# A fused transformer block on Trainium2: in its cross-attention stage, scores placed right behind attention, and one attention block moved into the next step

## The chip, the cores and the metric

One NeuronCore of a Trainium2 chip runs the whole block as one program. The metric is the device time of the program in microseconds (us); lower is better. Several executions of the kernel before were timed, and one more was recorded by the hardware profiler.

## The reference, cut to what matters

The block has three stages, each added to x (64 batches of 64 tokens, 512 wide, all float32): cross-attention over a context of 512 tokens, self-attention with 16 heads, and a feed-forward layer with ternary weights.

```python
x = x + xattn(layernorm(x), ctx, ctx, mask, W_Q, W_K, W_V, W_O)
x = x + attn(layernorm(x), Wq, bq, Wk, bk, Wv, bv, Wo, bo)
x = x + ffn(layernorm(x), W1, b1, W2, b2)

def xattn(Q, K, V, mask, W_Q, W_K, W_V, W_O):   # 16 heads of 32
    q, k, v = Q @ W_Q.T, K @ W_K.T, V @ W_V.T   # split into heads
    e = einsum('bhqd,bhkd->bhqk', q, k) / sqrt(32)
    e = where(mask, -inf, e)                    # mask: True is left out
    a = einsum('bhqk,bhkd->bhqd', softmax(e), v)
    return a @ W_O.T
```

The mask given leaves only keys of the last 128 of each batch's 512, and the kernel finds this out at run time (a flag) and then works with the last tile of 128 keys alone. The change is in the cross-attention stage; the other two stages are the same before and after.

## The kernel before, in words

**Tiling.** The cross stage has 16 units of 4 batches (4 x 64 = 256 tokens, two tiles of 128). A step `step(u, kind)` finishes the attention of unit u and, beside it, projects keys, values and queries of the next unit v = u+1. Steps 0 to 14 do both (`more` is true); step 15, the last, has no next unit. `run_steps` (L107) writes steps 0, 1, 14 and 15 out and runs the others as a loop of two steps a round.

**Precision.** Every projection is done with operands split into a high and a low part, so one output bank (128x512) takes 12 matmuls: 4 chunks of the contraction by the products hi*hi, hi*lo and lo*hi (`split_products`, whose matmul is L331). They are called here K0 to K3 (keys), V0 to V3 (values, one a batch), Q0 and Q1 (queries, 24 narrower matmuls each) and O0 and O1 (output projections of unit u's two tiles). They share two PSUM banks `project` in turn; a fixed list of names (`Banks`, with `full` at L437 and below) says which use gets which bank, and each use waits until the last use of its bank has been read out (`pj_free`).

**The attention of one batch q** goes through all compute engines:

- TensorE `scores(u, q)`, L581: 32-row tiles, 16 matmuls in the program (32 records in the trace), into PSUM `scores`.
- VectorE `maxima(u, q)`: adds the mask into SBUF (L842, which frees the PSUM), row maxima (L847), the bias of the exponential (L852).
- ScalarE `exponentials(u, q)`, L730: eight exponentials with row sums.
- VectorE `divide(u, q)`, L397 and L401: reciprocal of the sums and one product over 128x1024.
- TensorE `transposes(u, q)`, L590: eight transpositions into `probs_t_psum`.
- ScalarE `probs_t_out(u, q)`, L741: copy to SBUF.
- TensorE `attend(u, q)`, L607: 32-column tiles, into `attended_t`. Batches 0 and 1 fill tile 0, batches 2 and 3 tile 1.
- per tile, ScalarE `a_hi` (L715) and VectorE `a_lo` (L827) split the attended tile, TensorE does O0 or O1, VectorE `residual` (L864) adds it to x, and SyncE stores it (L515).

**Order.** There is no scheduler: each engine has its own list of calls in `step`, done strictly in that order, and semaphores tie them together. On TensorE (L620) one full step before is:

```
scores 0, O1 of u-1, K0, scores 1, K1, transposes 0, K2, attend 0, K3, scores 2,
V0, transposes 1, V1 with scores 3 in its middle, attend 1, V2, transposes 2,
O0, attend 2, Q0, transposes 3, Q1, attend 3, V3
```

On VectorE (L874): maxima 0, residual of O1 (u-1), divide 0, maxima 1, statistics of the next x, divide 1, `x_lo`, maxima 2, values_out V0, maxima 3, values_out V1, divide 2, a_lo 0, values_out V2, divide 3, residual of O0, split of the context of u+2, a_lo 1, values_out V3. `values_out` (L833) empties the bank of a V projection. On ScalarE (L750): exponentials 0, keys_out 0 and 1, probs_t_out 0, exponentials 1, keys_out 2, `x_hi`, keys_out 3, probs_t_out 1, exponentials 2, a_hi 0, exponentials 3, probs_t_out 2, split of the context, queries_out 0, probs_t_out 3, queries_out 1, a_hi 1. SyncE (L485) loads context and x^T of u+2, stores the two finished tiles, and then loads x of u+2 (L475) once the stores have landed, since both use the same buffer. GpSimd only works out the scale of the logits.

Of the kernel before, what the change touches and what calls it, by code (L numbers as in the profile page):

```python
# [43 lines left out]
def later(u, n):  # L44
    return Unit(u.half, u.off + n)
# [10 lines left out]
def is_unit(u, n):  # L56
    return isinstance(u.half, int) and number(u) == n
# [62 lines left out]
def build(nc, x, x_t, ctx, mask, w_cross, w_self, bq, bk, bv, bo, w1, b1, w2, b2,  # L120
# [4 lines left out]
    with outer:  # L125
# [261 lines left out]
        def self_w_lo(e, n):  # L387
            e.wait_ge(sw_hi_ready, n + 1)
            nc.vector.tensor_tensor(flat_w(sw_lo, n), s_stages[n],
                                    flat_w(sw_hi, n).bitcast(F32), ALU.subtract) \  # L390
                .then_inc(sw_lo_ready, 1)
# [143 lines left out]
        def cross_pe(e, K):  # L535
# [84 lines left out]
            def step(u, kind):  # L620
                more, ahead = kind != "last", kind == "full"
                v = later(u, 1)

                if is_unit(u, 0):
                    bank, before = K.banks.at(None, "Q1")
                else:
                    bank, before = K.banks.at(later(u, -1), "Q1",
                                              "last_but_one" if kind == "last" else "full")
                e.wait_ge(C.pj_free[bank], before + 1)
                scores(u, 0)  # L630
                if is_unit(u, 0):

                    e.wait_ge(w_lo_ready, 4)
                else:

                    o_proj(later(u, -1), K.nt - 1, "last_but_one" if kind == "last" else "full")
                if more:
                    k_proj(u, v, 0)
                scores(u, 1)
                if more:  # L640
                    k_proj(u, v, 1)
                    transposes(u, 0)
                    k_proj(u, v, 2)
                    attend(u, 0)
                    k_proj(u, v, 3)
                    scores(u, 2)
                    v_proj(u, v, 0)
                    transposes(u, 1)
                    v_proj(u, v, 1, lambda: scores(u, 3))
                    attend(u, 1)  # L650
                    v_proj(u, v, 2)
                    transposes(u, 2)
                    if K.nt == 2:
                        o_proj(u, 0, kind)
                    attend(u, 2)
                    q_proj(u, v, 0)
                    transposes(u, 3)
                    q_proj(u, v, 1)
                    attend(u, 3)
                    v_proj(u, v, 3)  # L660
                else:
                    scores(u, 2)
                    transposes(u, 0)
                    scores(u, 3)
                    attend(u, 0)
                    transposes(u, 1)
                    attend(u, 1)
                    transposes(u, 2)
                    if K.nt == 2:
                        o_proj(u, 0, kind)  # L670
                    attend(u, 2)
                    transposes(u, 3)
                    attend(u, 3)
                    o_proj(u, K.nt - 1, kind)
# [21 lines left out]
        def cross_act(e, K):  # L696
            def full(u, name, kind="full"):

                bank, before = K.banks.at(u, name, kind)
                wait(e, C.pj_full[bank], before + 1)  # L700
                return bank

            def keys_out(u, v, m):
                bank = full(u, f"K{m}")
                nc.scalar.activation(ck_t[:, parity(v), m, :, :].rearrange("p j k -> p (j k)"),
                                     PJ[bank][:], ACT.Copy).then_inc(C.pj_free[bank], 1)

            def x_hi(v):
                wait(e, xt_in, total(v, 16 * K.b, 16 * K.b))
                flat = lambda a: a[:, 0:K.b].rearrange("p b c s -> p (b c s)")  # L710
                nc.scalar.activation(flat(cxt_hi), flat(cxt_raw), ACT.Copy).then_inc(C.xt_hi, 1)

            def a_hi(u, t):
                wait(e, C.pv_done, total(u, 4, 4 // K.nt * (t + 1)))
                nc.scalar.activation(cat_hi[:, :, 0:K.tp], K.attended_t(t), ACT.Copy) \  # L715
                    .then_inc(C.at_hi, 1)

            def queries_out(u, n):

                bank = full(u, f"Q{n}")  # L720
                chunks = PJ[bank][:].rearrange("p (i b s) -> p i b s", i=2, s=SEQ)
                nc.scalar.activation(cq_t[:, 2 * n:2 * n + 2, 0:K.b, :], chunks[:, :, 0:K.b, :],
                                     ACT.Copy).then_inc(C.pj_free[bank], 1)

            def exponentials(u, q):
                wait(e, C.s_bias, total(u, 4, q + 1))
                width, buf = K.kt * P, q % 2
                for g in range(PAIRS // K.kt):
                    cols = slice(g * width, g * width + width)
                    last = nc.scalar.activation(  # L730
                        c_p[buf][:, cols], c_s[buf][:, cols], ACT.Exp,
                        bias=exp_bias[:, buf, g:g + 1],
                        scale=logit_scale[:, parity(u), K.batch(q):K.batch(q) + 1],
                        accum_out=c_row_sum[:, buf, g:g + 1])
                last.then_inc(C.p_ready, 1)

            def probs_t_out(u, q):
                wait(e, C.pt_full, total(u, 4, q + 1))

                wait(e, C.pv_done, total(u, 4, q))  # L740
                nc.scalar.activation(c_pt[:], PT[:], ACT.Copy).then_inc(C.pt_ready, 1)  # L741

            def split_ctx(v):

                wait(e, ctx_in[parity(v)], total_of_parity(v, 64, 64))
                nc.scalar.activation(ctx_hi[:, parity(v)].rearrange("p j c k -> p (j c k)"),
                                     ctx_raw[:, parity(v)].rearrange("p j c k -> p (j c k)"),
                                     ACT.Copy).then_inc(ctx_hi_ready, 1)

            def step(u, kind):  # L750
                more, ahead = kind != "last", kind == "full"
                v = later(u, 1)
                exponentials(u, 0)
                if more:
                    keys_out(u, v, 0)
                    keys_out(u, v, 1)
                probs_t_out(u, 0)
                exponentials(u, 1)
                if more:
                    keys_out(u, v, 2)  # L760
                    x_hi(v)
                    keys_out(u, v, 3)
                probs_t_out(u, 1)
                exponentials(u, 2)
                if K.nt == 2:
                    a_hi(u, 0)
                if not more:
                    self_w_hi(e, 0)
                    probs_t_out(u, 2)
                exponentials(u, 3)  # L770
                if more:
                    probs_t_out(u, 2)
                else:
                    self_w_hi(e, 1)
                if ahead:
                    split_ctx(later(u, 2))
                if more:
                    queries_out(u, 0)
                else:
                    self_w_hi(e, 2)  # L780
                probs_t_out(u, 3)
                if more:
                    queries_out(u, 1)
                a_hi(u, K.nt - 1)

            first = Unit(0, 0)
            split_ctx(first)
            cross_w_hi(e, 1)
            keys_out(None, first, 0)
            keys_out(None, first, 1)  # L790
            x_hi(first)
            keys_out(None, first, 2)
            keys_out(None, first, 3)
            cross_w_hi(e, 2)
            cross_w_hi(e, 3)
            queries_out(None, 0)
            queries_out(None, 1)
            split_ctx(later(first, 1))
            run_steps(e, K.units, step)

        def cross_dve(e, K):
# [72 lines left out]
            def step(u, kind):  # L874
                more, ahead = kind != "last", kind == "full"
                v = later(u, 1)
                maxima(u, 0)
                if not is_unit(u, 0):
                    residual(later(u, -1), K.nt - 1, "last_but_one" if kind == "last" else "full")
# [36 lines left out]
                if not more:  # L916
                    self_ln_statistics(e, Unit(0, 0))
                    e.wait_ge(G.stats, NT)
                    self_ln_normalise(e, Unit(0, 0))
                a_lo(u, K.nt - 1)  # L920
                if more:
                    values_out(u, v, 3)
                else:
                    self_w_lo(e, 2)
                    residual(u, K.nt - 1, kind)

# [884 lines left out]
```

## Time and profile before

| | before |
|---|---|
| median of 3 runs | 1789.76 us (1788.92 to 1798.7) |
| profiled execution | 1789.14 us |
| its span, first to last instruction | 1787.3 us |
| mean granted TensorE clock | 0.981 |
| TensorE busy | 1697.0 us, 95% |
| TensorE weight load busy | 1424.1 us, 80% |
| VectorE busy | 1030.4 us, 58% |
| ScalarE busy | 703.0 us, 39% |
| GpSimd busy | 205.4 us, 11% |

The time of an execution is a little longer than its span (1789.14 against 1787.3 us), because the span begins at the first instruction and ends with the last. The cross stage takes some 784 us of it, self-attention up to about 1150, the feed-forward layer the rest. In the rows, PE is TensorE's matmul, PEld its weight load, DVE VectorE, ACT ScalarE, POOL GpSimd and SPq SyncE's DMA queue. A timeline row has start and length in us, the engine, the line of the kernel, the operation, output<-inputs, shapes and count, and in brackets the engine's idle time before it with what ended that. The chain of work that ended last follows the program back from its last instruction, at each step to what released it, or else to the instruction before it on its engine.

### The profile page before, as it was taken

The page shows a single profiled execution, that of the slowest core. Times are in us where ns is not written, and L with a number is a line of the kernel's source. Part 1 is how long each engine was busy: PE and PEld are TensorE (multiplying, and loading weights), DVE is VectorE, ACT ScalarE, POOL GpSimd, SP SyncE. Part 2 cuts the span into 40 slices and gives each one's busy share as a digit, 9 for nine tenths or more (in the row PEclk, how much of TensorE's full clock was granted, in tenths as well). Part 3 has the DMA queues.
Part 4 walks back from the last instruction along what each step waited for, and adds up shares of the span by engine and source line. Part 5 has one row for each costly group of instructions (what it writes and reads, how often), then busy time and mean ns, then how long its engine had stood idle before and what let it go on. Part 6 is the DMA issues. An engine that isn't in the chain of part 4 may idle for free.

```text
span 1787.3 us, 38867 instructions
## 1 busy us (share of the span) xinstructions
PE 1697.0 (95%) x16268; PEld 1424.1 (80%) x16268; DVE 1030.4 (58%) x1494; ACT 703.0 (39%) x1689; POOL 205.4 (11%) x298
## 2 busy tenths in 40 slices
PE   6899999999999999769999999999699999999999
PEld 4788878888888788558889888988578888888887
DVE  3655555555555555546677776778654455445533
ACT  3555555555555555536422222222122222222221
POOL 1000000000000000011112121211121022102200
PEclk9999999999999999879999999999799999999999
DMA  5011111111111111241010101000211011101000
GB/s 213 13 60 61 60 61 60 61 60 61 60 61 60 61 60 72 95 189 50 25 50 25 47 26 43 32 25 34 66 36 48 1 48 48 47 0 47 24 24 24
DMA packets 48695, 95.45 MB, mean 53 GB/s; under 512 B 5792, under 2 KB 14112, under 8 KB 47264
## 3 DMA queue, kind: packets, MB, share of 16 engines
q1 hardware_dynamic: 48544, 93.16, 14.9%
q8 instruction: 128, 2.10, 0.5%
q14 instruction: 23, 0.19, 0.0%
HBM read 67.97 MB, written 25.17 MB: 52 GB/s over the span
## 4 chain that ended last, share of the span: by engine, by line
PE 90%; DVE 4%; issue 2%; ACT 2%; DMA 1%; SPq 0%; DVEq 0%; POOL 0%; ACTq 0%
PE project L331 50%; PE project L1548 13%; PE scores L581 4%; PE probs_t_psum L590 3%; PE scores L1562 3%; PE scores L1564 3%; PE probs_t_psum L1564 3%; PE probs_t_psum L1562 3%; PE attended_t L607 2%; PE probs_t_psum L1137 2%; PE scores L1127 1%; PE attended_t L1156 1%; PE attended_t L1015 1%; DVE ff_weight_scratch L1402 1%; PE project L1096 1%
## 5 line engine op out<-in xcount | busy, mean ns | idle before, releaser
L1548 PE MATMUL project<-ff_xt,w_ternary 128*128 128x512 f32 x1024 | 255.9, 392 | 1.7 <-DVE ff_xt L1027 1.7
L1548 PEld LDWEIGHTS project<-ff_xt,w_ternary 128*128 128x128 f32 x1024 | 190.0, 188 | 40.3 <-issue 1.9
L1597 ACT ACTIVATE hidden<-project,b_sb 128x512 f32<-128x512 f32 x128 | 88.3, 690 | 325.3 <-PE project L1548 324.0
L1622 DVE CAST hidden_hi<-hidden 128x512 fp32r<-128x512 f32 x128 | 56.8, 444 | 229.7 <-ACT hidden L1597 228.8
L730 ACT ACTIVATE cross_scores_probs<-cross_scores_probs,exp_bias,logit_scale 128x128 f32<-128x128 f32 x256 | 122.8, 485 | 103.0 <-DVE exp_bias L852 103.0
L331 PE MATMUL project<-self_xt_hi,self_w_hi 128*128 128x256 f32 x512 | 149.4, 292 | 2.3 <-DVE self_xt_lo L1340 2.3
L331 PE MATMUL project<-self_xt_lo,self_w_hi 128*128 128x256 f32 x512 | 146.3, 286 | 0.0
L331 PE MATMUL project<-self_xt_hi,self_w_lo 128*128 128x256 f32 x512 | 146.2, 286 | 0.0
L730 ACT ACTIVATE cross_probs<-cross_scores,exp_bias,logit_scale 128x128 f32<-128x128 f32 x256 | 122.8, 484 | 0.0
L331 PE MATMUL project<-ctx_hi,cross_w_hi 128*128 128x512 f32 x256 | 106.6, 417 | 14.8 <-DVE ctx_lo L871 14.8
L331 PE MATMUL project<-cross_w_hi,ctx_hi 128*128 128x512 f32 x256 | 108.7, 425 | 0.0
L331 PEld LDWEIGHTS project<-self_xt_hi,self_w_hi 128*128 128x128 f32 x512 | 99.8, 195 | 4.7 <-issue 2.8
L331 PE MATMUL project<-ctx_lo,cross_w_hi 128*128 128x512 f32 x256 | 101.5, 396 | 0.0
L331 PE MATMUL project<-ctx_hi,cross_w_lo 128*128 128x512 f32 x256 | 101.4, 396 | 0.0
L331 PE MATMUL project<-cross_w_hi,ctx_lo 128*128 128x512 f32 x256 | 100.7, 393 | 0.0
L331 PE MATMUL project<-cross_w_lo,ctx_hi 128*128 128x512 f32 x256 | 100.3, 392 | 0.0
L331 PEld LDWEIGHTS project<-self_xt_lo,self_w_hi 128*128 128x128 f32 x512 | 99.8, 195 | 0.6
L1564 PE MATMUL probs_t_psum<-w_ternary,hidden_lo 128*128 128x512 f32 x256 | 99.7, 390 | 0.0
L331 PEld LDWEIGHTS project<-self_xt_hi,self_w_lo 128*128 128x128 f32 x512 | 99.7, 195 | 0.0
L1562 PE MATMUL scores<-w_ternary,hidden_hi 128*128 128x512 f32 x256 | 99.6, 389 | 0.0
L1564 PE MATMUL scores<-w_ternary,hidden_lo 128*128 128x512 f32 x256 | 99.6, 389 | 0.0
L1562 PE MATMUL probs_t_psum<-w_ternary,hidden_hi 128*128 128x512 f32 x256 | 99.6, 389 | 0.0
(158 smaller groups left out, 3823.3 us busy)
## 6 DMA issues: line engine op xcount, KB each, us to landing
ctx_raw<-in_ctx SPq DMA_DIRECT2D x64, 256.0 KB, 3.9
cross_xt_raw<-in_x_t SPq DMA_DIRECT2D x64, 128.0 KB, 2.2
cross_x<-in_x SPq DMA_DIRECT2D x32, 256.0 KB, 3.0
x<-cross_x SPq DMA_DIRECT2D x32, 256.0 KB, 2.0
self_x<-x SPq DMA_DIRECT2D x32, 256.0 KB, 2.9
ff_w_raw<-in_w SPq DMA_DIRECT2D x2, 4096.0 KB, 18.3
x<-self_residual SPq DMA_DIRECT2D x32, 256.0 KB, 2.0
ff_x<-x SPq DMA_DIRECT2D x32, 256.0 KB, 3.7
```

Source lines behind the costliest of these rows:

```text
L331: last = nc.tensor.matmul(out_ap, a, b, start=(n == 0), stop=(n == 3 * len(pairs) - 1))
L581: last = nc.tensor.matmul(S[half:half + SEQ, slot * n:(slot + 1) * n], cq_t[rows, c, K.batch(q), :], keys, start=True, stop=True)
L590: last = nc.tensor.transpose(PT[:, i * P:i * P + P], c_p[q % 2][:, i * P:i * P + P], ident[:])
L607: last = nc.tensor.matmul(PV[rows, t, col:col + SEQ], cv[:, parity(u), q if K.kt == 1 else k, DK * head:DK * head + DK], c_pt[:, at:at + S ...
L730: last = nc.scalar.activation(c_p[buf][:, cols], c_s[buf][:, cols], ACT.Exp, bias=exp_bias[:, buf, g:g + 1], scale=logit_scale[:, parity(u ...
L1015: last = nc.tensor.transpose(XB[t % 2][:, c * P:c * P + P], fxn[:, t % 2, c * P:c * P + P], ident[:])
L1137: last = nc.tensor.transpose(PT[:, i * P:i * P + P], s_p[:, i * P:i * P + P], ident[:])
L1548: last = nc.tensor.matmul(PJ[m % 2][:], w1_q[:, c, cols], x_t[parity(v)][:, c, :], start=(c == 0 and x_t is fxt_hi), stop=(c == DC - 1 and ...
L1562: nc.tensor.matmul(YB[t], h_hi[:, m % 4, rows], w2_q[:, m, :], start=(m == 0), stop=False)
L1564: last = nc.tensor.matmul(YB[t], h_lo[:, m % 4, rows], w2_q[:, m, :], start=False, stop=(m == FC - 1))
L1597: nc.scalar.activation(h_raw[:, m % 2, :], PJ[m % 2][:], ACT.Relu, bias=b1_sb[:, m:m + 1]).then_inc(h_relu, 1)
L1622: nc.vector.tensor_copy(h_hi[:, m % 4, :], h_raw[:, m % 2, :]).then_inc(h_hi_ready, 1)
```

## The change

On TensorE, `scores 2` moves from behind K3 to right behind `attend 0`, and `scores 3` from the middle of V1 to right behind `attend 1`. `attend 3` of unit u leaves step u and becomes the first thing of step u+1, ahead of its `scores 0`; V3 now follows Q1 directly. K0 and O1 of the unit before change places, so that K0 stands between `scores 0` and O1. On ScalarE and VectorE, `a_hi 1` and `a_lo 1` of unit u move along, to the head of step u+1. The orders of the two engines are otherwise as before, the list of banks too, and SyncE's and GpSimd's programs are untouched. The last step keeps its own order for all that it does for unit 15. A full step on TensorE is then:

```
attend 3 of u-1, scores 0, K0, O1 of u-1, scores 1, K1, transposes 0, K2, attend 0,
scores 2, K3, V0, transposes 1, V1, attend 1, scores 3, V2, transposes 2, O0,
attend 2, Q0, transposes 3, Q1, V3
```

```diff
--- before.py
+++ after.py
@@ -627,27 +627,30 @@
                     bank, before = K.banks.at(later(u, -1), "Q1",
                                               "last_but_one" if kind == "last" else "full")
                 e.wait_ge(C.pj_free[bank], before + 1)
+                if not is_unit(u, 0):
+                    attend(later(u, -1), 3)
                 scores(u, 0)
+                if more:
+                    k_proj(u, v, 0)
                 if is_unit(u, 0):
 
                     e.wait_ge(w_lo_ready, 4)
                 else:
 
                     o_proj(later(u, -1), K.nt - 1, "last_but_one" if kind == "last" else "full")
-                if more:
-                    k_proj(u, v, 0)
                 scores(u, 1)
                 if more:
                     k_proj(u, v, 1)
                     transposes(u, 0)
                     k_proj(u, v, 2)
                     attend(u, 0)
+                    scores(u, 2)
                     k_proj(u, v, 3)
-                    scores(u, 2)
                     v_proj(u, v, 0)
                     transposes(u, 1)
-                    v_proj(u, v, 1, lambda: scores(u, 3))
+                    v_proj(u, v, 1)
                     attend(u, 1)
+                    scores(u, 3)
                     v_proj(u, v, 2)
                     transposes(u, 2)
                     if K.nt == 2:
@@ -656,7 +659,6 @@
                     q_proj(u, v, 0)
                     transposes(u, 3)
                     q_proj(u, v, 1)
-                    attend(u, 3)
                     v_proj(u, v, 3)
                 else:
                     scores(u, 2)
@@ -750,6 +752,8 @@
             def step(u, kind):
                 more, ahead = kind != "last", kind == "full"
                 v = later(u, 1)
+                if not is_unit(u, 0):
+                    a_hi(later(u, -1), K.nt - 1)
                 exponentials(u, 0)
                 if more:
                     keys_out(u, v, 0)
@@ -781,7 +785,8 @@
                 probs_t_out(u, 3)
                 if more:
                     queries_out(u, 1)
-                a_hi(u, K.nt - 1)
+                else:
+                    a_hi(u, K.nt - 1)
 
             first = Unit(0, 0)
             split_ctx(first)
@@ -874,6 +879,8 @@
             def step(u, kind):
                 more, ahead = kind != "last", kind == "full"
                 v = later(u, 1)
+                if not is_unit(u, 0):
+                    a_lo(later(u, -1), K.nt - 1)
                 maxima(u, 0)
                 if not is_unit(u, 0):
                     residual(later(u, -1), K.nt - 1, "last_but_one" if kind == "last" else "full")
@@ -917,10 +924,10 @@
                     self_ln_statistics(e, Unit(0, 0))
                     e.wait_ge(G.stats, NT)
                     self_ln_normalise(e, Unit(0, 0))
-                a_lo(u, K.nt - 1)
                 if more:
                     values_out(u, v, 3)
                 else:
+                    a_lo(u, K.nt - 1)
                     self_w_lo(e, 2)
                     residual(u, K.nt - 1, kind)
```

## Rows read from the trace of the kernel before

**Rows 1.** The page: busy time by engine, and the chain that ended last by engine.

```profile
PE 1697.0 (95%) x16268; PEld 1424.1 (80%) x16268; DVE 1030.4 (58%) x1494; ACT 703.0 (39%) x1689; POOL 205.4 (11%) x298
...
PE 90%; DVE 4%; issue 2%; ACT 2%; DMA 1%; SPq 0%; DVEq 0%; POOL 0%; ACTq 0%
```

**Rows 2.** One step by stretches: length; PE, PEld, DVE, ACT, POOL busy (count); clock; DMA; GB/s.

```profile
237.14:281.98 44.84, 44.84 (x460) 36.48 (x457) 26.37 (x35) 26.58 (x78) 3.14 (x6) 1.00 0.19 60
```

**Rows 3.** The chain in that step: start, length (us), engine, piece.

```profile
237.21 5.68 PE project L331 x24
...
247.76 2.73 PE project L331 x12
...
251.08 2.94 PE project L331 x12
...
255.06 2.96 PE project L331 x12
...
258.89 1.39 PE project L331 x6
...
261.31 1.59 PE project L331 x6
262.90 0.58 PE attended_t L607 x32
263.49 2.96 PE project L331 x12
```

**Rows 4.** TensorE timeline: batch 2's transpositions, and O0's first matmul behind them.

```profile
266.28 1.04 PE L590 MATMUL probs_t_psum<-ident,cross_scores_probs 128*128 128x128 f32 x8
267.07 0.48 PE L331 MATMUL project<-cross_w_hi,cross_at_hi 128*128 128x512 f32 x1
```

**Rows 5.** VectorE timeline behind batch 3's scores; brackets: idle before, releaser.

```profile
261.38 1.23 DVE L842 TENSOR_TENSOR cross_scores<-scores,mask_bias 128x1024 f32<-128x1024 f32 x1 [2.63 <-PE scores L581]
...
264.04 0.68 DVE L833 COPY cross_v<-project 128x512 f32<-128x512 f32 x1
...
264.86 1.22 DVE L401 TENSOR_TENSOR cross_scores_probs<-cross_scores_probs,cross_row_scale 128x1024 f32<-128x1024 f32 x1
266.01 0.68 DVE L827 TENSOR_TENSOR cross_at_lo<-attended_t,cross_at_hi 128x512 fp32r<-128x512 f32 x1
```

**Rows 6.** The last step's chain: division, hand-over, transpositions.

```profile
757.37 1.23 DVE cross_scores_probs L401
758.61 0.14 issue
```

**Rows 7.** ScalarE timeline: batch 2's transposed probabilities copied out.

```profile
268.01 1.01 ACT L741 ACTIVATE cross_probs_t<-probs_t_psum 128x1024 f32<-128x1024 f32 x1
```

**Rows 8.** VectorE timeline: low half of the second attention tile.

```profile
278.73 0.69 DVE L827 TENSOR_TENSOR cross_at_lo<-attended_t,cross_at_hi 128x512 fp32r<-128x512 f32 x1 [5.59 <-ACT cross_at_hi L715]
```

**Rows 9.** VectorE timeline: O1's residual, batch 0's product, batch 1's reciprocal.

```profile
240.21 0.69 DVE L864 TENSOR_TENSOR cross_x<-project,cross_x 128x512 f32<-128x512 f32 x1
...
244.36 1.23 DVE L401 TENSOR_TENSOR cross_scores_probs<-cross_scores_probs,cross_row_scale 128x1024 f32<-128x1024 f32 x1
...
252.68 0.20 DVE L397 RECIPROCAL cross_row_scale<-cross_row_sum 128x8 f32<-128x8 f32 x1 [2.92 <-ACT cross_probs L730]
```

**Rows 10.** SyncE timeline: the next loads of x.

```profile
243.36 0.83 SPq L475 DMA_DIRECT2D cross_x<-in_x  x2
```

**Rows 11.** The page, DMA issues: x's load, size, us to landing.

```profile
cross_x<-in_x SPq DMA_DIRECT2D x32, 256.0 KB, 3.0
```

**Rows 12.** TensorE timeline: two waits ahead of the steady part.

```profile
46.58 0.35 PE L331 MATMUL project<-cross_xt_hi,cross_w_hi 128*128 128x256 f32 x1 [2.09 <-DVE cross_w_lo L376]
...
57.46 0.77 PE L331 MATMUL project<-ctx_hi,cross_w_hi 128*128 128x512 f32 x1 [3.11 <-DVE ctx_lo L871]
```

**Rows 13.** The stretches behind those two waits (columns as in rows 2).

```profile
46.50:53.00 6.50, 5.99 (x48) 5.81 (x48) 2.77 (x2) 1.00 (x2) 0.00 (x0) 1.00 0.00 0
57.40:65.00 7.60, 7.54 (x50) 5.80 (x51) 3.50 (x5) 4.41 (x17) 0.00 (x0) 0.68 0.01 2
```

## The prediction

> **What bounds the kernel now.** I begin with the page: TensorE is busy for 95% of the span and makes up 90% of the chain that ended last, so only what shortens or stops TensorE counts [rows 1]. Then one step of the cross stage by stretches: from the first matmul of one O1 to that of the next it takes 44.84 us, and TensorE is busy in all 44.84 of them, at a granted clock of 1.00, while VectorE has 26.37 and ScalarE 26.58 [rows 2]. TensorE waits for nobody there. So two questions decide: how much TensorE time the new order saves, and whether each thing that TensorE takes from VectorE and ScalarE is still ready when its new place comes. The chain in that step answers the first, the VectorE timeline the second [rows 3, 5].
>
> **What the new order saves.** The number of matmuls is the same. What differs is how often TensorE passes from the full-size projections to the small tiles of scores or attention and back. The chain shows what that costs. A group of 12 between transpositions and an attention takes 2.73 us; the groups that follow a block of small tiles take 2.94 to 2.96; two groups with nothing between them take 5.68, where K3 and V0, with scores 2 between them, take 2.94 + 2.96 = 5.90 [rows 3]. So placing scores 2 behind attend 0 saves 5.90 - 5.68 = 0.22 us. V1 in two pieces takes 1.39 + 1.59 = 2.98; whole, between the transpositions and attend 1, it is the 2.73 of K2: 0.25 saved [rows 3]. For attend 3 behind V3 and ahead of scores 0 no row stands alone, and I take the mean of the two, 0.24. What passing from attention straight to scores costs no row shows. I take attention's 0.58 and the 1.03 of scores (from 258.89 + 1.39 = 260.28 to 261.31) as they are [rows 3], so nothing extra; the bounds are that a merge saves nothing, and that it saves twice the 0.23 by which 2.96 exceeds 2.73, that is 0.46. I stay with 0.24, since the 5.68 against 5.90 is measured on the very blocks that become neighbours. Three merges a unit, 15 units (steps 0 to 14 hold the inner two, the heads of steps 1 to 15 the third): 45 x 0.24 = 10.8 us saved, were nothing else touched.
>
> A rule speaks against this size. The Trainium skill, "TensorEngine Tiling (Array Packing)", section Tiling Modes, Key Properties, says that a change of tiling mode drains the engine, and that moving to another tile of the same mode doesn't. Attention (128x32) and scores (32x64) are two modes, so by it the boundary between them is still a switch, and of four switches three remain; the saving would be nearer to half of mine, some 5 us in all, and the forecast some 5 us later. The trace of before has no such boundary at this clock to tell; nothing below hangs on it.
>
> **Where TensorE will be stopped.** Moving scores 3 back is the edit that costs. Count from the start of V1's piece at 258.89. Scores 3 follows there after 1.39 us; in the new order after the whole V1 and attend 1, 2.73 + 0.58 = 3.31 [rows 3]. It comes 1.92 us later. VectorE stood idle for 2.63 us until those scores arrived (its row at 261.38), so everything queued behind them moves by the full 1.92: the mask addition and maxima, V1's copy (264.04), then the reciprocal and the product of batch **2** (264.86, ending 266.08), and a_lo of tile 0 (266.01) [rows 5]. The product is not late for want of data: it is queued behind the maxima of batch 3, and the change leaves VectorE's order there alone. Transpositions 2 need this product. They started at 266.28 [rows 4], 0.20 after its end, and the last step shows the hand-over taking 0.14 [rows 6]: there were 0.06 us to spare. Now the product ends at 266.08 + 1.92 = 268.00, and the transpositions start at 268.14, which is 1.86 later than before. TensorE, with V1 whole, would have been ready at 266.28 - 0.25 = 266.03, so it stands idle for 2.11 us in every full step, and V2 with its 2.96 us is all that covers the 5 us of VectorE's work.
>
> **What else is moved, and what covers it.**
> - Tile 0's O0 follows the transpositions 0.79 later (267.07 against 266.28) [rows 4]. Its a_lo ends at 266.69 + 1.92 = 268.61, with the hand-over 268.75, and O0 can start at 268.93: 0.18 to spare [rows 5]. V1's bank, which O0 takes, is free 2 us before that.
> - Exponentials 3 start with the bias, 1.92 later, so the copy behind them, which attend 2 needs, ends at 269.02 + 1.92 = 270.94 [rows 7]. Attend 2 comes a projection after 268.93, at 271.85. It would have been the next to be late (by 1.2 us) had the transpositions not been held already.
> - Scores 2 come 2.94 us earlier. VectorE can't use that: its maxima 2 stand behind batch 1's division. Nothing, and their PSUM is free since maxima 1.
> - Head of the step: a_lo 1 now stands ahead of maxima 0 on VectorE, and a_hi 1 ahead of exponentials 0 on ScalarE. a_lo takes 0.69 behind a_hi [rows 8]; together with a_hi, about as long, and the hand-overs they end some 1.4 to 1.5 us after attend 3. Scores 0 need 1.03, so maxima 0 and its successors slip by 0.3. What covers this is the room ahead of transpositions 0: batch 0's product ended at 244.36 + 1.23 = 245.59 [rows 9], and they, some 0.9 us long, ended where K2's piece begins, at 247.76 [rows 3]; so they began near 246.8 and had about 1 us to spare. O1 has K0 and scores 0 in front, 3.9 us against 1.5: no wait. K0 needs V3's bank copied out (0.69) and has attention and scores before it, 1.6: no wait.
> - K1 takes O1's bank and now has only scores 1 (1.03) between them. The residual takes 0.69 [rows 9], with the hand-overs about 0.9. No wait, but little room: 0.1 us. If it fails, it costs up to 0.3 a unit.
> - SyncE stores that tile about 2.9 us later, so x of u+2 is asked for 2.9 later as well: the second of the loads begun at 243.36 lands 3.0 us after its issue [rows 10, 11], before near 247, after near 250. VectorE's statistics wait for it, and behind them stands batch 1's division, which has idled until 252.68 for ScalarE anyway [rows 9]: covered. The context loads go out behind it with 15 us in hand.
> - Last step: there is no K0, so O1 of unit 14 has only scores 0 (1.03) to cover the 1.5 us of a_hi and a_lo: 0.45 us once.
>
> **The sum.** A full step: 1.86 (transpositions 2, in which V1's saving is already counted) - 0.22 - 0.24 = +1.40 us. Times 15, 21.0; with the last step 21.4. Against the profiled execution, 1789.14 + 21.4 = 1810.5 us. That execution is 0.6 us under the median of the runs shown, so the forecast carries over to the median. This is +1.2%. Something over 0.5% (9 us) is about what a measurement of this kernel can tell from no change: under 1780.8 is faster, above 1798.7 slower.
>
> **The rivals.**
> 1. *No hold, the merges alone* (the other side). If the product of batch 2 were in time after all, the savings stand alone: 1789.1 - 10.8 = 1778.3. For it: no row of the steady part has TensorE waiting at transpositions 2. Against: the product is behind the scores in program order, and only 0.06 us are spare [rows 4 to 6]. It decides at a lateness of 0.7 us per unit; I work out 1.9. Chance 0.05.
> 2. *A partial hold, near no change.* If the scores came only half as late (VectorE's idle 2.63 us partly soaking it up, or dearer passages in the old order than the chain shows), 15 x 0.0 to 0.6: 1785 to 1798. Chance 0.05.
> 3. *The clock falls in each hold.* After the wait of 3.11 us at 57.46, which had a first one shortly ahead of it, the stretch behind ran at a granted 0.68 of the full 2.4 GHz; after the single wait of 2.09 us at 46.58, with projections on both sides, it stayed at 1.00 [rows 12, 13]. My hold of 2.11 us has projections before it and is nearest to the second. Should the clock fall every time, 7.60 x (1 - 0.68) = 2.4 us a unit are lost, 36 in all: 1847; in some units only, in between. Chance 0.08. The Trainium skill, "TensorE: Matmul & The Clock Gate", section Part 1, has the gate lower the clock after idleness and raise it by sustained work; by this rule a longer idle stretch each unit is a danger, and the two rows show one case of each kind.
> 4. *K1 held as well.* Residual of O1 late by 0.1 to 0.6 us a unit: 1812 to 1820. Chance 0.07, within the range.
> 5. *The passage from attention to scores costs what a merge saves:* 10.8 us more, 1821. Within my own case's range.
>
> My forecast has 0.75. Its own range runs from merges at 0.46 (10 us less, 1801) to merges at nothing (1821). Both ends are unlikely, so 1802 to 1822 holds the main case, the fourth and a clock that falls in a few units; outside are the first two and most of the third, under 2 in 10. Faster 0.05, within 0.5% 0.05, slower 0.90.
>
> **What would show it.** In the profile of the changed kernel: a full step of about 46.2 us in place of 44.84; about 2.1 us of idle ahead of transpositions 2 ended by VectorE's product (L401), in 15 steps, some 31 us in all, and none of weight elsewhere in the steady part; V1 as one piece of 2.73, K3 and V0 as one of 5.68; the granted clock at 1.00. It is wrong if transpositions 2 don't wait; if attend 2, O0 or K1 wait instead; or if the stretch behind the hold shows a granted clock under 1.

## The result, and the profile after

The changed kernel takes 1828.71 us (median of 4 runs, 1827.08 to 1834.34) against 1791.45 us for the kernel before beside it: a ratio of 1.0207 with a 95% interval of 1.0169 to 1.0245. The forecast was 1810.5 us, 1802 to 1822: the direction was right, the size was not, and the time lies outside the range. The profiled execution took 1827.08 us, its span is 1825.3 us.

The page of the changed kernel, with busy times, the granted clock in 40 slices, and the chain by engine:

```profile
PE 1705.2 (93%) x16268; PEld 1436.9 (79%) x16268; DVE 1028.4 (56%) x1494; ACT 704.2 (39%) x1689; POOL 217.8 (12%) x298
...
PEclk9999999999999999969999999999889999999999
...
PE 86%; DVE 8%; issue 2%; ACT 2%; DMA 1%; SPq 0%; DVEq 0%; POOL 0%; ACTq 0%
```

Against [rows 1], TensorE's share of the chain has gone from 90% to 86% and VectorE's from 4% to 8%: there are now stretches in which TensorE waits for VectorE. TensorE's busy time has grown as well, by 8.2 us (1697.0 to 1705.2), though the number of matmuls is the same, 16268. So there are two losses, one of waiting and one of slower work: the mean granted clock fell from 0.981 to 0.971.

The chain through one step (start, length in us, engine, piece) shows the first:

```profile
211.28 1.03 PE scores L581 x32
212.31 5.67 PE project L331 x24
...
218.85 2.76 PE project L331 x12
221.62 0.58 PE attended_t L607 x32
222.20 1.08 PE scores L581 x32
...
223.30 1.23 DVE cross_scores L847
...
224.56 1.23 DVE cross_row_max L852
...
225.81 0.23 DVE exp_bias L857
226.05 0.59 DVE cross_v L838
226.64 0.12 DVE cross_row_scale L397
...
226.78 1.23 DVE cross_scores_probs L401
228.01 0.14 issue
228.15 1.06 PE probs_t_psum L590 x8
229.21 2.75 PE project L331 x12
```

It answers to [rows 3, 5]. K3 and V0 are one piece of 5.67 us, V1 one of 2.76, and attention passes to scores 3 at 0.58 us, as foreseen. Then TensorE's V2, which follows scores 3, is no longer in the chain. In its place stands VectorE's whole queue: mask addition, maxima, bias, V1's copy, reciprocal, and the product of batch 2, with the hand-over of 0.14, and then the transpositions.

TensorE's waits in the cross stage:

```profile
PE probs_t_psum L590 <- DVE cross_scores_probs L401: 31.5, 16, 2.0
PE probs_t_psum L590 <- DVE cross_probs L401: 3.6, 1, 3.6
PE project L331 <- DVE ctx_lo L876: 3.1, 1, 3.1
PE attended_t L607 <- issue: 1.7, 4, 0.5
PE scores L581 <- DVE cross_scores L847: 1.3, 1, 1.3
PE attended_t L607 <- ACT cross_probs_t L743: 1.1, 1, 1.1
PE scores L581 <- ACT cross_q_t L724: 0.7, 1, 0.7
PE project L331 <- DVE cross_at_lo L832: 0.5, 1, 0.5
```

The first row is the hold (TensorE's wait for VectorE's product ahead of transpositions 2): 16 waits, 15 of them of 1.97 or 1.98 us in the 15 full steps, and one of the last step. Nothing else waits in the steady part except at the heads of some rounds of the loop (`issue`), which the kernel before had too. O0, attend 2 and K1 don't wait.

The second loss is in the stretch behind the hold. TensorE's timeline behind the hold at 274.93, and then the granted clock behind two holds (columns as in rows 2, the clock third from the right):

```profile
274.93 1.45 PE L590 MATMUL probs_t_psum<-ident,cross_scores_probs 128*128 128x128 f32 x8 [1.98 <-DVE cross_scores_probs L401]
276.02 0.78 PE L331 MATMUL project<-cross_w_hi,cross_at_hi 128*128 128x512 f32 x1
276.60 0.63 PE L331 MATMUL project<-cross_w_lo,cross_at_hi 128*128 128x512 f32 x1
277.02 0.63 PE L331 MATMUL project<-cross_w_hi,cross_at_lo 128*128 128x512 f32 x1
...
278.73 0.47 PE L331 MATMUL project<-cross_w_hi,cross_at_hi 128*128 128x512 f32 x1
279.04 0.40 PE L331 MATMUL project<-cross_w_lo,cross_at_hi 128*128 128x512 f32 x1
279.27 0.40 PE L331 MATMUL project<-cross_w_hi,cross_at_lo 128*128 128x512 f32 x1
```

```profile
228.10:232.00 3.90, 3.85 (x28) 3.11 (x32) 2.53 (x4) 3.90 (x10) 0.00 (x0) 1.00 0.00 0
...
274.90:281.00 6.10, 6.07 (x53) 4.90 (x54) 3.12 (x6) 4.59 (x10) 0.00 (x0) 0.72 0.01 3
275.60:278.80 3.20, 3.20 (x11) 2.62 (x10) 1.81 (x3) 3.20 (x8) 0.00 (x0) 0.50 0.02 5
```

After the hold that ends at 228.15 the clock stays at 1.00 and O0 takes 2.75 us. After the one that ends at 274.93 the mean over the stretch is 0.72: matmuls are 0.42 us apart (276.60 to 277.02) in place of 0.23 (279.04 to 279.27), with the granted clock at 0.50 (from 275.6 to 278.8), the 1.2 GHz level, until about 278.9; from 279.0 on it is 1.00 again, 2.4 GHz. From the start of the transpositions to attend 2, a step without a fall takes 3.75 us and a step with one 5.35: a fall of the clock costs 1.6 us. In this execution it happened in 9 of the 15 full steps.

How the cross stage ends is read from the first transposition of the self stage, which does the same thing in all kernels (first and last start are the two times with "to"). Before:

```profile
L1096 PE MATMUL project<-ident,self_x_norm x128: 270/272/477, 784.4 to 1234.3; 128*128 128x128 f32 x128
```

and after:

```profile
L1103 PE MATMUL project<-ident,self_x_norm x128: 270/272/474, 821.2 to 1268.8; 128*128 128x128 f32 x128
```

The cross stage is 821.2 - 784.4 = 36.8 us longer, and the whole span 38.0. Nine falls make 9 x 1.6 = 14.4 us of that, which leaves 22.4, against the 21.4 of the forecast's sum. The parts are told apart better by the step: an undisturbed one takes 46.29 to 46.31 us from transpositions 2 to transpositions 2 in place of 44.84, 1.46 more where the forecast has 1.40. That makes 21.9 us in 15 steps. Outside the steps the stage's first transposition comes 1.5 us later than before (68.0 against 66.5), and the waits at the heads of the loop's rounds are shorter (1.7 against some 3.5 us); neither was in the forecast, and they nearly cancel.

### The profile page after: what moved, and what is told of

It is laid out like the page before. It is cut to its first block, busy times and chain, and to the rows that moved or that the text cites. A ratio compares the mean times of both kernels' runs of the same rounds, so it can differ in the third digit from the quotient of the medians.

```text
span 1825.3 us, 38880 instructions
## 1 busy us (share of the span) xinstructions
PE 1705.2 (93%) x16268; PEld 1436.9 (79%) x16268; DVE 1028.4 (56%) x1494; ACT 704.2 (39%) x1689; POOL 217.8 (12%) x298
## 4 chain that ended last, share of the span: by engine, by line
PE 86%; DVE 8%; issue 2%; ACT 2%; DMA 1%; SPq 0%; DVEq 0%; POOL 0%; ACTq 0%
PE project L331 47%; PE project L1555 13%; PE probs_t_psum L590 3%; PE scores L581 3%; PE scores L1569 3%; PE scores L1571 3%; PE probs_t_psum L1571 3%; PE probs_t_psum L1569 3%; PE attended_t L607 2%; PE probs_t_psum L1144 2%; PE scores L1134 1%; DVE cross_scores_probs L401 1%; DVE cross_scores L847 1%; DVE cross_row_max L852 1%; PE attended_t L1163 1%
## 5 line engine op out<-in xcount | busy, mean ns | idle before, releaser
L838 DVE COPY cross_v<-project 128x512 f32<-128x512 f32 x64 | 43.7, 685 | 117.4 <-PE project L331 117.4
L331 PE MATMUL project<-cross_w_hi,ctx_hi 128*128 128x512 f32 x256 | 103.5, 404 | 0.0
```

The lines of the kernel that those rows point to most:

```text
L331: last = nc.tensor.matmul(out_ap, a, b, start=(n == 0), stop=(n == 3 * len(pairs) - 1))
L838: nc.vector.tensor_copy(cv[:, parity(v), j, :], PJ[bank][:]) \
```

## The experiments

Each kernel is the changed one, or the one before, with the edit shown. "Cross stage" is the time of that first transposition in the kernel's profile; "falls" are the full steps in which the time from transpositions 2 to attend 2 is 5.3 to 5.4 us instead of 3.75.

### Undoing and isolating scores 3

The changed kernel, scores 3 put back:

```diff
-                    v_proj(u, v, 1)
+                    v_proj(u, v, 1, lambda: scores(u, 3))
                     attend(u, 1)
-                    scores(u, 3)
```

> The changed kernel with scores 3 put back into the middle of V1; the two other merges stay. Theory (the late scores make the hold of 2.0 us at transpositions 2, and the idleness lets the clock fall in 9 of 15 steps): no hold, granted clock 1.00 in every step, a step of about 44.84 - 0.46 = 44.4 us, in all 1789 - 15 x 0.46 + 0.45 (last step) = 1783 us. Rival (blocks of small tiles back to back lower TensorE's activity, and the clock falls for that): the other two merges are there, so clock falls go on, some 1.6 us each, and the time stays above 1797.

Measured: 1787.08 us beside a before of 1796.86, ratio 0.9945 (0.9924 to 0.9966); cross stage 777.5 against 784.4, 6.9 less. Steps take 44.35 us, 0.49 less than before, where the forecast's terms for these two merges give 0.22 + 0.24 = 0.46. TensorE's waits, from 60 to 740 us, where only the last row but one is of the loop and the others belong to the last step:

```profile
PE probs_t_psum L590 <- DVE cross_scores_probs L401: 1.9, 1, 1.9
PE scores L581 <- DVE cross_scores L846: 1.3, 1, 1.3
PE attended_t L607 <- issue: 0.8, 2, 0.5
PE project L331 <- DVE cross_at_lo L831: 0.5, 1, 0.5
```

No hold and no fall. The two merges that remain are faster than the order before, and blocks of small tiles side by side don't by themselves lower the clock.

The other way round, the kernel before with scores 3 moved and nothing else:

```diff
-                    v_proj(u, v, 1, lambda: scores(u, 3))
+                    v_proj(u, v, 1)
                     attend(u, 1)
+                    scores(u, 3)
```

> The kernel before with one edit: scores 3 right behind attend 1. Theory: hold of about 2.1 us in each of 15 steps, a step 1.86 us longer, 28 us in all, plus clock falls as in the changed kernel (9 x 1.6 = 14): about 1832 us, nearly all of the loss from this edit. Rival (the hold needs the moved attend 3 or scores 2 as well): hold under 1 us and under 1805. If only the falls need the other edits: 1817 with a granted clock of 1.00.

Measured: 1831.64 us, ratio 1.0196 (1.0179 to 1.0213); hold 1.97 to 1.98 in all 15 steps, 6 falls, cross stage 822.7. This one edit carries the loss. By 15 x 1.86 + 6 x 1.6 the stage would be 37.5 us longer than before; it is 38.3.

### Taking idle time out of the hold

VectorE copies V1 out first, so the queue behind scores 3 is shorter:

```diff
+                    values_out(u, v, 1)
                     maxima(u, 3)
-                    values_out(u, v, 1)
```

> The changed kernel with VectorE copying V1 out ahead of maxima 3 in place of behind it. VectorE's queue behind scores 3 gets 0.60 us shorter, so the hold goes from 1.98 to about 1.4 us: 15 x 0.6 = 9 us less. If the clock falls depend on how long TensorE idles, they get rarer or vanish: 1827 - 9 - 14 = about 1804, clock 1.00. If they come whatever the length: about 1818.

```profile
499.76 1.06 PE L590 MATMUL probs_t_psum<-ident,cross_scores_probs 128*128 128x128 f32 x8 [1.38 <-DVE cross_scores_probs L401]
```

Measured: hold 1.38 in each step, no falls, cross stage 796.1, profiled execution 1800.17 us. The median of its 7 runs is higher, 1807.69 (1800.17 to 1814.29), ratio 1.0066 (1.0043 to 1.0089). Its cross stage is 25.1 us shorter than the changed kernel's: 9 of it the 0.6 us a step, 14.4 the falls, and most of the rest shorter waits at the heads of the loop's rounds (0.4 against 1.7 us). What the runs above 1807 lost is not in the profile, which is of the fastest; their mean granted clock is lower (0.976 to 0.980 against 0.981), so TensorE ran slowly for longer there; in which stage isn't known.

The same hold filled with work that isn't needed:

```diff
                     v_proj(u, v, 2)
+                    wait(e, C.pt_ready, total(u, 4, 2))
+                    for _ in range(8):
+                        nc.tensor.matmul(PT[:, 0:512], ctx_hi[:, parity(v), 2, 0, :],
+                                         cw_hi[:, 2, 0, :], start=True, stop=True)
                     transposes(u, 2)
```

> The changed kernel with 8 useless full-size matmuls (about 8 x 0.23 = 1.8 us) in the hold ahead of transpositions 2; they write a PSUM bank that the transpositions overwrite, so the result is the same. Theory (idleness lets the clock fall, and that is what the forecast lacked): hold left about 0.2 us, clock 1.00 in every step, steps no longer than an undisturbed step of the changed kernel, 1827 - 9 x 1.6 = about 1813 us. Rival (the clock falls for the small tiles, or the loss is something else than the clock): time stays at 1827 or goes up by what the filler adds.

TensorE's timeline at one hold: the filler, the transpositions, O0's first matmul.

```profile
320.52 1.98 PE L657 MATMUL probs_t_psum<-cross_w_hi,ctx_hi 128*128 128x512 f32 x8
322.66 1.06 PE L590 MATMUL probs_t_psum<-ident,cross_scores_probs 128*128 128x128 f32 x8 [0.17 <-DVE cross_scores_probs L401]
323.49 0.48 PE L331 MATMUL project<-cross_w_hi,cross_at_hi 128*128 128x512 f32 x1
```

Measured: 1808.42 us, ratio 1.0061 (1.0043 to 1.0078), 0.17 us of idleness left and no falls. A kernel with 120 more matmuls is 20 us faster than the changed one. Its cross stage ends at 811.2, 10.0 us sooner: 14.4 for the falls that are gone, less 4.4 that come in anew (below the table). The other 8 us or so are gained in the two later stages, which the edit doesn't touch, most of it in self-attention, where three waits of TensorE at scores with no releaser (`issue`), 5.1 us in the changed kernel, are missing. What the filler is worth is therefore read from the cross stage. The step is as long as an undisturbed one of the changed kernel, 46.3 us (276.37 to 322.66), so nothing waits less for the result; in the cross stage only the clock is kept. This separates the two losses: the time given to waiting for VectorE is all there, and the slower work behind it is gone.

### How long, and what around it

A wait of about the same length made by delay alone, in the kernel with scores 3 back:

```diff
                     values_out(u, v, 1)
+                    for i, n in enumerate((512, 512, 512, 192)):
+                        nc.vector.reduce_max(counts[:, i:i + 1], mask_bias[:, 0:n], AXIS.X)
```

> Kernel e1 (scores 3 in V1's middle, no hold, no clock falls) with four useless reductions of about 2.1 us on VectorE ahead of the division of batch 2: the same wait of about 2.0 us at transpositions 2, made by delay alone, with scores 3 not next to attend 1. If idleness is what lets the clock fall: 15 x 2.0 = 30 us more than e1 plus falls in some half of the steps (8 to 15 us): 1787 + 30 + 12 = about 1829, granted clock about 0.97 and rows of a stretched O0. If the block of attend 1 and scores 3 ahead of V2 is needed for it: no falls, about 1817.

```profile
274.92 1.06 PE L590 MATMUL probs_t_psum<-ident,cross_scores_probs 128*128 128x128 f32 x8 [1.84 <-DVE cross_scores_probs L401]
275.74 0.47 PE L331 MATMUL project<-cross_w_hi,cross_at_hi 128*128 128x512 f32 x1
276.05 0.39 PE L331 MATMUL project<-cross_w_lo,cross_at_hi 128*128 128x512 f32 x1
```

Measured: 1812.4 us, ratio 1.0106 (1.008 to 1.0133), no falls, cross stage 807.0. On its face this is what the second theory expected. But the idle time came out at 1.83 to 1.84 us and not at 2.0, so it didn't tell the two apart. The changed kernel with a single filler matmul (`range(1)`) ran beside it:

> The changed kernel with one useless matmul (0.23 us) in the hold, so that TensorE idles about 1.75 us there in place of 1.98, and the step stays as long. If falls get rarer as the idle time shrinks (none at 1.38 in the profile of e3, 9 of 15 at 1.98): some 3 to 6 falls, 1827 - 1.6 x (3 to 6) = about 1818 to 1823. If they are a matter of all or nothing at a given length: either 1827 or 1813.

```profile
274.96 1.07 PE L590 MATMUL probs_t_psum<-ident,cross_scores_probs 128*128 128x128 f32 x8 [1.75 <-DVE cross_scores_probs L401]
```

Measured: hold 1.75, **no** falls, cross stage 806.2, within 1 us the changed kernel's 821.2 less its falls. Here the block of attend 1 and scores 3 is in place, so the block alone doesn't make the clock fall. The total nevertheless was 1834.79 us (ratio 1.0236, 1.021 to 1.0261), higher than the changed kernel's: in its profile the self stage, which no edit touches, has TensorE waiting 10 times, 20.9 us in all, at scores with no releaser (`issue`), where the kernel before has 3 such waits of 6.1 us, and a granted clock of 0.90 to 0.94 in five of the six stretches of 50 us from 956 to 1256, where the changed kernel's has 1.00 (871 to 1221). The two come together. These waits come in five pairs, each wait 1.2 to 2.7 us long and the two of a pair some 4 us apart, and behind each pair the clock is at 0.50 (956.6 to 962.0 and 1156.7 to 1163.3, for two), whereas in the kernel before single waits of 1.70 and 1.79 us leave it at 1.00 and only the third, of 2.66, is followed by a fall (0.50 from 1113.7 to 1117.0). So what this stage loses, 28 us against the kernel before, is again idle time with slow work behind it; why there are more waits isn't known. Judged by its total, this run would have misled; the stage's own end has to be read.

The delay kernel with the last reduction at 352 columns in place of 192:

> As the last run of this kind, with the last useless reduction longer, so that TensorE idles about 2.00 us at transpositions 2 in place of 1.84, with scores 3 in V1's middle. If the length of the idle time decides (none at 1.75 and 1.84, 9 of 15 at 1.98): clock falls are back in several steps, cross stage about 807 + 15 x 0.16 + 10 to 20 = 820 to 829 us. If the block of attend 1 and scores 3 is needed besides: no stretched O0, cross stage about 809.

One step's transpositions and attend 2, and then the stretches behind a hold with a fall and one without:

```profile
230.80 1.17 PE L590 MATMUL probs_t_psum<-ident,cross_scores_probs 128*128 128x128 f32 x8 [2.00 <-DVE cross_scores_probs L401]
...
236.12 0.65 PE L607 MATMUL attended_t<-cross_probs_t,cross_v 128*32 128x64 f32 x32
```

```profile
230.70:236.20 5.50, 5.40 (x25) 4.29 (x29) 2.48 (x4) 2.82 (x2) 0.00 (x0) 0.69 0.01 3
184.20:188.00 3.80, 3.73 (x20) 3.01 (x20) 2.45 (x4) 2.63 (x2) 0.00 (x0) 1.00 0.02 4
```

Measured: 1830.17 us, ratio 1.0209 (1.0182 to 1.0236), hold 2.00, falls in 9 of 15 steps, cross stage 824.5. Adding 0.16 us of idleness made the stage 17.5 us longer, 15 x 0.16 = 2.4 by itself and 14.4 by falls. The executions that weren't profiled agree: the mean granted clock is 0.978 to 0.982 in all four runs with 1.84 us and 0.970 to 0.973 in all five with 2.00. The length of the idle time decides, and the neighbourhood of attend 1 and scores 3 isn't needed.

Does more idleness mean more falls?

```diff
                     values_out(u, v, 1)
+                    nc.vector.reduce_max(counts[:, 0:1], mask_bias[:], AXIS.X)
```

> The changed kernel with one useless reduction of 0.6 us on VectorE ahead of the division of batch 2: TensorE idles about 2.58 us. Cross stage longer by 15 x 0.6 = 9 us for the delay; and if more idleness means more clock falls, in 12 to 15 of 15 steps and each of 1.6 us or more: 821 + 9 + 5 to 12 = 835 to 842 us. If the number of falls doesn't grow with the length: about 830.

Measured: 1831.15 us, ratio 1.0225 (1.0196 to 1.0253), hold 2.57, falls in 7 of 15, cross stage 822.6. The first expectation fell: the number doesn't grow with the length. An undisturbed step is 0.6 us longer, 46.90 for 46.29, as it should be; that the stage isn't longer as a whole comes from fewer falls, from shorter waits at the heads of rounds, and from an earlier first step (its transpositions 2 start at 87.67 against 89.26, though they are held 0.6 longer).

And the changed kernel again, unedited:

> The changed kernel once more, unedited, beside the two others. Theory: hold 1.98 us in every step again, and stretched transpositions or O0 in several steps, though not always the same ones; number of falls between 6 and 12 of 15, cross stage 816 to 826 us. Rival (the falls of the first profile were an accident of that execution): none or few falls, and about 1813 us.

Measured: 1829.4 us, ratio 1.0211 (1.0183 to 1.0238), hold 1.98, falls in 12 of 15 steps, cross stage 823.0. So the falls are no accident of the first profile, but which steps they hit is.

The profiles so far together (idle time at transpositions 2, falls, end of the cross stage):

| kernel | idle, us | falls of 15 | cross stage, us |
|---|---|---|---|
| before | 0 | 0 | 784.4 |
| scores 3 back | 0 | 0 | 777.5 |
| filler of 8 | 0.17 | 0 | 811.2 |
| V1's copy first | 1.38 | 0 | 796.1 |
| filler of 1 | 1.75 | 0 | 806.2 |
| delay, scores 3 back | 1.84 | 0 | 807.0 |
| scores 3 alone | 1.98 | 6 | 822.7 |
| changed, first profile | 1.98 | 9 | 821.2 |
| changed, again | 1.98 | 12 | 823.0 |
| longer delay, scores 3 back | 2.00 | 9 | 824.5 |
| changed, 0.6 us more delay | 2.57 | 7 | 822.6 |

The filler of 8 ends about 4 us later than the sum gives, and its profile has the reason: 4.6 us of waits with no releaser at its projections, in 5 of the rounds.

### A version faster than both

The hold can be covered with work that is needed. Q0 depends on nothing of batch 2 or 3:

```diff
-                        + ["O0"] * two + ["Q0", "Q1", "V3", f"O{self.nt - 1}"])
+                        + ["Q0"] + ["O0"] * two + ["Q1", "V3", f"O{self.nt - 1}"])
...
                     v_proj(u, v, 2)
+                    q_proj(u, v, 0)
                     transposes(u, 2)
...
                     attend(u, 2)
-                    q_proj(u, v, 0)
...
+                    values_out(u, v, 1)
                     maxima(u, 3)
-                    values_out(u, v, 1)
```

> The changed kernel with Q0 placed between V2 and transpositions 2 (bank list Q0 before O0 to match) and VectorE copying V1 out ahead of maxima 3. Q0 is 3.0 us of full-size work that needs nothing of batch 2 or 3, against a hold of 1.98 us: theory: no hold, all three merges kept, clock 1.00, a step of 44.84 - 0.74 = 44.1 us, in all 1789 - 11 + 0.5 = 1779 us, ratio to before about 0.994. Rival (something else of the new order is late next: attend 2, transpositions 3 or Q1's bank): some other wait of TensorE of 0.3 us or more in each step, and no gain over e1.

The chain in one step, attend 1 to O0, all of it TensorE's:

```profile
259.27 0.58 PE attended_t L607 x32
259.85 1.03 PE scores L581 x32
260.89 5.82 PE project L331 x36
266.70 0.87 PE probs_t_psum L590 x8
267.58 2.75 PE project L331 x12
```

Measured: 1779.15 us beside a before of 1792.26, ratio 0.9927 (0.9908 to 0.9947). V2 and Q0 are one piece of 5.82 us between scores 3 and the transpositions, no hold, no falls, cross stage 772.8. A step takes 44.09 us (from 138.49 to 182.58 at the transpositions) against 44.84: all three merges are kept. The 0.75 us can't be put down to the merges alone, since Q0's place has changed too: attend 2 now passes straight to transpositions 3. V1's copy goes first because Q0 takes V1's bank; without that the order wasn't tried.

## Why the prediction was wrong

**The merges: right.** K3 with V0 takes 5.67 us, V1 whole 2.76, attention passes to scores at 0.58, and the kernel with two of the merges, scores 3 back, has a step 0.49 us shorter, against the 0.46 of the forecast's terms. The third, V1 whole, is worth somewhat less than its 0.25: moving scores 3 lengthens the step by 46.30 - 44.35 = 1.95 us, where the idle time, counted as in the next paragraph, is 2.13, so 0.18 is saved. The rule that the prediction cites from the Trainium skill, "TensorEngine Tiling (Array Packing)", section Tiling Modes, Key Properties, was read there as leaving about half of the saving. The trace doesn't bear that size out: the boundary of attention and scores costs about what I took, and the merges of scores 2 and scores 0 are worth 0.49 together.

**The hold: right.** Product of batch 2 late behind maxima 3, 2.11 us of waiting foreseen, 1.98 measured, in each of 15 steps; the small difference is that a matmul's modelled end runs some 0.15 us past what I counted as TensorE being ready (by that count it is 2.13). Scores 3 alone bring it and putting them back removes it.

**What was said to be covered: right.** O0, attend 2, K1 and the statistics don't hold TensorE. The last step's O1 waits 0.5 us for a_lo, as foreseen (0.45).

**The sum of these: right, and its closeness in part luck.** 21.4 us foreseen; the changed kernel's cross stage less its falls is 22.4 longer, and the run with one filler, which has the same steps and no falls, 21.8. The second profile of the changed kernel gives 823.0 - 784.4 - 12 x 1.6 = 19.4: the start of the stage and the heads of the rounds move such a figure by 2 or 3 us. The step, 1.46 us longer against 1.40, is the firmer check.

**The clock: wrong, and this is the step that failed.** The sum has no term for it. The forecast put the single wait of 2.09 us at 46.58 beside the hold and concluded that the clock would stay at 1.00 [rows 12, 13]; the falling clock was given a chance of 0.08. It fell in 9 of 15 steps, at 1.6 us each 14.4 us in all, and in 12 in the second profile. Two things were wrong in the reading. One row at each side was taken for a rule, where the wait of 2.09 us was a single draw: in the runs above, holds of 1.98 to 2.57 us left the clock alone in 32 of 75 steps, so a single wait that passes without a fall says little, and fifteen of them in one program say much. And the price was read off a stretch behind a longer idleness, at 2.4 us; a fall here costs 1.6. With 9 falls of 1.6 us added to its own sum, the forecast would have said 1825, near the 1827.08 of the profiled execution.

The Trainium skill, "TensorE: Matmul & The Clock Gate", Part 1, describes a gate that follows how busy the engine has been and that isn't in step with the kernel; that the same hold falls in some steps and not in others agrees with it. Its advice in "Why this matters for your kernels" is to avoid idle gaps longer than the ones here; here gaps of 1.98 us were enough, in 27 of 45 steps.

**Left open.** Why the falls don't get more frequent from 1.98 to 2.57 us; whether anything between 1.84 and 1.98 is a sharp edge or only a change of odds (no kernel was held for a time in between, and the four lengths below were profiled once each); and what brings TensorE's waits with no releaser at the heads of loops, which made the self stage of the run with one filler 28 us longer and that of the run with eight shorter.

## What to carry to other kernels

When an instruction is moved later on the bounding engine, follow it into the queue of the engine that consumes it: everything behind the consumer moves too, and here the sixth item of VectorE's queue, of another batch, was due with 0.06 us to spare. Once a periodic wait is found, price it twice, as idle time and as slower work behind it, and don't let one undisturbed wait in the trace excuse it: here 2 us of waiting cost another 1 us on average. And where such a hold can't be avoided, move needed work into it, as Q0 here; even useless matmuls were better than idling (the cross stage ended 10.0 us sooner).

## What the runs showed that I had not expected

A filler of 120 useless matmuls made the cross stage 10.0 us shorter (821.2 to 811.2), by keeping the clock. Lengthening a recurring wait from 1.84 to 2.00 us made the cross stage 17.5 us longer. Lengthening it on from 1.98 to 2.57 us cost nothing as a whole: the delay made each undisturbed step 0.6 us longer, but with 7 falls in place of 9 or 12 the stage ended at 822.6 us, about where it had with 1.98.
